# Preparing the edge slots of a message-passing layer: conversion loop without chunk restarts, paired records, transposes on TensorE

## The reference

```python
for l in range(5):
    h = leaky(x @ W1[l] + b1[l]) @ W2[l] + b2[l]
    e = leaky(edge_attr @ We1[l] + be1[l]) @ We2[l] + be2[l]
    msg = h[src] * e * dot_scale[l]
    agg = segment_sum(msg, dst, num_segments=n)
    x = layernorm(x + agg * res_w[l]) * ln_g[l] + ln_b[l]
```

## Time and profile before

| what | value |
|---|---|
| median of 3 runs | 6804.82 us (6796.08 to 6816.65) |
| the profiled execution's own time | 6786.73 us, its span 6784.7 us |
| busy in the span | PE 85%, PEld 56%, DVE 76%, ACT 17%, POOL 67% |
| TensorE clock granted, mean | 0.884 of 2.4 GHz |
| conversion stage | from 799.8 us (first fetch) to 1290.9 us (first load of the layers) |

### The profile page before, as it was taken

The page is one execution under the profiler, slowest core; times in us unless marked ns, Lnnn a source line. Parts: engine busy times, 40 slices in busy tenths (PEclk is TensorE's granted clock), DMA queues, the critical chain, the costliest instruction groups (busy, mean ns, idle before and its releaser), DMA issues.

```text
span 6784.7 us, 172226 instructions
## 1 busy us (share of the span) xinstructions
PE 5734.0 (85%) x64844; PEld 3820.2 (56%) x64845; DVE 5152.1 (76%) x7991; ACT 1160.8 (17%) x1852; POOL 4527.7 (67%) x4793
## 2 busy tenths in 40 slices
PE   6776888888888888988878988887888887888887
PEld 2223443456666655666655666665566665556665
DVE  8997533588877678877758887766887775888886
ACT  0000232211111111111111111211111122111111
POOL 5777777466666457766737776754777672777775
PEclk8997566899989889999979999997999997999998
DMA  3112388755556445555635555553555563556664
GB/s 132 25 25 49 92 212 210 185 134 135 139 136 148 115 113 127 145 136 142 149 84 136 139 139 142 148 136 91 133 141 137 144 149 89 137 145 148 156 172 111
DMA packets 733557, 886.39 MB, mean 131 GB/s; under 512 B 325488, under 2 KB 502976, under 8 KB 731568
## 3 DMA queue, kind: packets, MB, share of 16 engines
q1 hardware_dynamic: 568480, 703.64, 39.7%
q0 software_dynamic: 152144, 154.93, 11.5%
q10 hardware_dynamic: 12096, 16.53, 0.8%
HBM read 749.51 MB, written 125.06 MB: 129 GB/s over the span
## 4 chain that ended last, share of the span: by engine, by line
PE 46%; issue 18%; DVE 16%; POOL 12%; DVEq 4%; ACT 3%; DMA 1%; ACTq 0%; SPq 0%; POOLq 0%
PE bank L976 14%; POOL slots L775 11%; PE bank L972 9%; PE bank L1025 7%; PE bank L1050 5%; DVE arena L1659 3%; PE bank L854 3%; PE bank L1012 3%; DVEq L1779 2%; DVE arena L1667 2%; DVE arena L1747 2%; ACT arena L1238 2%; PE bank L840 2%; DVE x_packed L1667 2%; DVE nodes_state L1715 2%
## 5 line engine op out<-in xcount | busy, mean ns | idle before, releaser
L788 POOL DMA_INDIRECT arena<-h_rows,src x3855 | 3676.5, 954 | 1798.9 <-issue 1258.4
L976 PEld LDWEIGHTS bank<-w2s,arena 128*128 128x128 f32 x8960 | 1188.5, 212 | 779.6 <-DVE arena L1747 421.8
L976 PE MATMUL bank<-w2s,arena 128*128 128x128 f32 x8960 | 1321.1, 305 | 201.0 <-DVE arena L1747 186.0
L775 POOL DMA_INDIRECT slots<-arena,slot_index x792 | 785.6, 992 | 267.1 <-issue 241.2
L972 PE MATMUL bank<-nodes_state,edge_w 64*128 64x512 f32 x980 | 617.9, 714 | 305.5 <-DVE nodes_state L1715 142.3
L1050 PEld LDWEIGHTS bank<-arena 112*64 112x64 f32 x20160 | 657.4, 141 | 269.2 <-issue 246.7
L1050 PE MATMUL bank<-arena 112*64 112x64 f32 x20160 | 744.0, 228 | 61.4 <-issue 55.3
L972 PE MATMUL bank<-x_packed,edge_w 64*128 64x512 f32 x1260 | 760.7, 686 | 16.9 <-ACT std L1187 15.9
L1238 ACT ACTIVATE arena<-bank,tenth 128x512 f32<-128x512 f32 x490 | 336.4, 687 | 2416.4 <-PE bank L972 2416.1
L1659 DVE SCALAR_TENSOR_TENSOR arena<-bank,edge_w,arena 128x512 f32<-128x512 f32 x490 | 366.6, 748 | 435.3 <-ACT arena L1238 430.4
L1667 DVE TENSOR_TENSOR x_packed<-bank,slot_rel 128x2880 f32<-128x2880 f32 (+8 forms) x315 | 588.8, 1869 | 15.9 <-issue 15.9
(11 more groups left out here) (198 smaller groups left out, 5811.7 us busy)
## 6 DMA issues: line engine op xcount, KB each, us to landing
arena<-slot_pick SPq DMA_DIRECT2D x630, 448.0 KB
arena<-h_rows SPq DMA_DIRECT2D x630, 224.0 KB
x_packed<-slot_attr SPq DMA_DIRECT2D x630, 128.0 KB
nodes_state<-attr_t SPq DMA_DIRECT2D x485, 128.0 KB
arena<-h_rows,src POOLq DMA_INDIRECT x3855
slot_pick<-arena SPq DMA_DIRECT2D x126, 448.0 KB
slots<-arena SPq DMA_DIRECT2D x9, 1904.0 KB, 22.1
arena<-slots SPq DMA_DIRECT2D x126, 136.0 KB
```

Of the source, the lines that this page charges most:

```text
L775: pool.indirect_dma_start(slots, bass.IndirectOffsetOnAxis(ap=slot_index[:, t:t + 1], axis=0), records[:, v, j, :], None).then_inc(record_ ...
L788: pool.indirect_dma_start(to[0:n, at:at + D], None, table, bass.IndirectOffsetOnAxis(ap=index[0:n, t:t + 1], axis=0)).then_inc(landed(t), 16)
L976: mm = pe.matmul(to[:, j * P:(j + 1) * P], acts[:, j * TILE:(j + 1) * TILE], w2s[:, :], start=True, stop=True)
```

## The change

The conversion runs through all 126 groups as one loop on SP and on PE. SP issues three fetches, then for each group `keep_hot(p)` and behind it the fetch of group p + 3; the wait for POOL's records stands ahead of the first fetch of each chunk. There are four record buffers in place of six. In a buffer the records have a pitch of 64 floats, with record j of side 0 and record j of side 1 next to each other, so that one 98-float slice holds both; a fetch is two DMAs of 512 records, one for each side. PE turns such a slice with one `transpose` of 128 x 98 into partitions 0 to 97, four for each group. ACT copies the 98 partitions with one instruction. DVE clears `msg` once at the start, since the gaps between records are now turned and copied as well.

```diff
-RECORD_BUFS = 6
+RECORD_BUFS = 4
+        PAIR = D + REC
+        slot_records = arena[:, records_at:records_at + RECORD_BUFS * HALF].rearrange(
+            "p (v j r) -> p v j r", v=RECORD_BUFS, r=P)
+        by_side = slot_records.rearrange("p v j (side r) -> p v side j r", side=2)
...
-                    sp.dma_start(slot_records[:, v, :, :],
-                                 slots[p * GROUP:(p + 1) * GROUP, :].rearrange("(t q) r -> q t r", q=TILE)
-                                 ).then_inc(slots_landed[v], 16)
+                    for side in range(2):
+                        at = p * GROUP + side * HALF
+                        sp.dma_start(by_side[:, v, side, :, 0:REC],
+                                     slots[at:at + HALF, :].rearrange("(j q) r -> q j r", q=TILE)
+                                     ).then_inc(slots_landed[v], 16)
...
-                    first_p, last_p = c * BG, (c + 1) * BG
-                    for p in range(first_p, first_p + RECORD_BUFS - 1):
-                        fetch(p)
-                    for p in range(first_p, last_p):
-                        if p + RECORD_BUFS - 1 < last_p:
-                            fetch(p + RECORD_BUFS - 1)
-                        keep_hot(p)
+                for p in range(RECORD_BUFS - 1):
+                    fetch_sent(p)
+                for p in range(NB):
+                    keep_hot(p)
+                    if p + RECORD_BUFS - 1 < NB:
+                        fetch_sent(p + RECORD_BUFS - 1)
...
                     for j in range(TPH):
-                        for side in range(2):
-                            mm = pe.matmul(turn_ps[p % 2][side * D:side * D + REC, j * TILE:(j + 1) * TILE],
-                                           slot_records[:, v, side * TPH + j, :], ident[:, :], start=True, stop=True)
+                        mm = pe.transpose(turn_ps[p % 2][0:PAIR, j * TILE:(j + 1) * TILE],
+                                          slot_records[:, v, j, 0:PAIR], ident[:, :])
                     mm.then_inc(turn_ready, 1)
...
-                for c in range(CHUNKS):
-                    turn(c * BG)
-                    for p in range(c * BG, (c + 1) * BG):
-                        if p + 1 < (c + 1) * BG:
-                            turn(p + 1)
-                        source_of(p)
+                turn(0)
+                for p in range(NB):
+                    if p + 1 < NB:
+                        turn(p + 1)
+                    source_of(p)
...
-                    for side in range(2):
-                        at = slice(side * D, side * D + REC)
-                        ins = act.activation(turned[at, p % 2, :], turn_ps[p % 2][at, :], ACT.Identity)
-                    ins.then_inc(turned_out, 1)
+                    act.activation(turned[0:PAIR, p % 2, :], turn_ps[p % 2][0:PAIR, :], ACT.Identity
+                                   ).then_inc(turned_out, 1)
...
+            dve.memset(area("msg"), 0.0)
...
-                    dve.tensor_copy(slot_rel[:, p * TPG:(p + 1) * TPG], slot_records[:, v, :, ED + 1]
-                                    ).then_inc(rel_taken, 1)
+                    dve.tensor_copy(slot_rel[:, p * TPG:(p + 1) * TPG].rearrange("p (side j) -> p side j", side=2),
+                                    by_side[:, v, :, :, ED + 1]).then_inc(rel_taken, 1)
```

More of the change, by code:

```diff
@@ L277, in build @@
         start_f = area("slot_pick", 2 * NG, 2 * NCA)
-        slot_records = arena[:, first_of["hid_tenth"]:first_of["hid_tenth"] + RECORD_BUFS * TPG * REC].rearrange(
-            "p (v t r) -> p v t r", v=RECORD_BUFS, r=REC)
+        PAIR = D + REC
+        records_at = first_of["hid_tenth"]
+        slot_records = arena[:, records_at:records_at + RECORD_BUFS * HALF].rearrange(
+            "p (v j r) -> p v j r", v=RECORD_BUFS, r=P)
+        by_side = slot_records.rearrange("p v j (side r) -> p v side j r", side=2)
+        assert records_at + RECORD_BUFS * HALF == total
         spill_records = spill_msg[:, 0:TPG * REC].rearrange("p (t r) -> p t r", r=REC)
@@ L615, in keep_hot, with fetch_sent @@
                     sp.dma_start(slot_pick[p, :, :], source_hot[0:ROWS, p % 2, :]).then_inc(hot_stored[p % 2], 16)
-                for c in range(CHUNKS):
[L618 to L623, removed]
-                    first_p, last_p = c * BG, (c + 1) * BG
-                    for p in range(first_p, first_p + RECORD_BUFS - 1):
-                        fetch(p)
-                    for p in range(first_p, last_p):
-                        if p + RECORD_BUFS - 1 < last_p:
-                            fetch(p + RECORD_BUFS - 1)
-                        keep_hot(p)
+                def fetch_sent(p):
+                    if p % BG == 0:
+                        n = records_of(p // BG)
+                        for v in range(2):
+                            sp.wait_ge(record_sent[v], 16 * REC_TILES * ((n + 1 - v) // 2))
+                        if p == (CHUNKS - 1) * BG:
+                            sp.dma_start(spill_records,
+                                         slots[SPILL:SPILL + GROUP, :].rearrange("(t q) r -> q t r", q=TILE)
+                                         ).then_inc(spill_landed, 16)
+                    fetch(p)
+                for p in range(RECORD_BUFS - 1):
[4 more added lines that the diff above has]
+                        fetch_sent(p + RECORD_BUFS - 1)
                 for v in range(2):
@@ L890, in turn @@
                     v = p % RECORD_BUFS
-                    pe.wait_ge(slots_landed[v], 16 * (p // RECORD_BUFS + 1))
+                    pe.wait_ge(slots_landed[v], 32 * (p // RECORD_BUFS + 1))
                     if p > 1:
@@ L1578, in turn_slots @@
                     v = p % RECORD_BUFS
-                    dve.wait_ge(slots_landed[v], 16 * (p // RECORD_BUFS + 1))
-                    dve.tensor_copy(slot_rel[:, p * TPG:(p + 1) * TPG], slot_records[:, v, :, ED + 1]
-                                    ).then_inc(rel_taken, 1)
+                    dve.wait_ge(slots_landed[v], 32 * (p // RECORD_BUFS + 1))
+                    dve.tensor_copy(slot_rel[:, p * TPG:(p + 1) * TPG].rearrange("p (side j) -> p side j", side=2),
+                                    by_side[:, v, :, :, ED + 1]).then_inc(rel_taken, 1)
                     if p > 1:
```

## The result

| | before | changed |
|---|---|---|
| median of 4 runs | 6800.73 us | 6906.02 us (6900.44 to 6924.61) |
| ratio | 1 | 1.0165, 95% interval 1.0136 to 1.0195 |
| profiled execution, own time | 6786.73 us | 6924.61 us |
| first to last `keep_hot` | 477.9 us | 616.8 us |
| clock granted, mean | 0.884 | 0.865 |

The account below looks back on a forecast made before the run. The conversion's loop was taken as the bound: PE at the low clock, DMA at the upper, plus restarts. Changed, 125 groups at 4.54 us add 86.6 us; with the memset, 6804.8 + 87.5 = 6892 us, range 6790 to 6955.

Parts of the forecast that it names:

- The loop, 9.09 us: Conversion: one-hots of p, store, fetch landing, turn, source matmuls, DVE, one-hots of p + 2; 9.09 us for two groups.
- Two of the signs: Expected in the changed trace: `keep_hot` at an even 4.5 us; PE idle for records before the transposes in nearly every group.
- The pace, 4.54 us: Conversion at the lower clock: 4.54 us a group, from 9.09 us for two, with a fetch landing in 4.11.
- Transposes, 0.97 us for four: PE's turn of a group: four transposes at 0.24 us each, 0.97 in all, bounds 0.48 and 1.89.
- ACT's copy at nothing: ACT in the conversion: one copy for two changes the time by 0, as the copy is covered by a whole turn.
- Restarts, -64 us: Eight chunk boundaries of the conversion: running on across them removes 64 us, if the pace inside the chunks stayed.
- Memset, +0.9 us: DVE's clearing of `msg` at the head of its chain adds 0.9 us.
- POOL's gate: SP's wait for POOL's records before a chunk's fetches costs nothing; it would bite below 3.05 us a group for chunk 6.
- The clock at 0.50: PE's clock in the conversion stays at its lower level, 0.50, through the whole stage.
- the one on the other side, faster: Rival: fetches land in 2.9 us and the clock is high, 3.23 us a group, -76 us, 6729 us; chance 0.16.
- The dear transposes: Rival: transposes cost as much as full matmuls, turn 1.89 us, 5.0 us a group, 6950 us; chance 0.13.
- the high clock: Rival: PE's clock stays high in the conversion, 3.84 us a group, 6805 us, no change; chance 0.13.

Follow-up runs that it names:

- a3_matmul: The changed kernel with the old eight identity matmuls and two ACT copies in place of the transposes: stage 635.0 us, ratio 1.0174 to the kernel before.
- a1_order: The changed kernel with fetch(p + 3) issued ahead of `keep_hot(p)`: stage 414.7 us, 3.32 a group, ratio 0.9935 to the kernel before.
- a7_warm: The changed kernel with three matmuls of no use added to each group on PE: stage 581.3 us, ratio 1.0115 to the kernel before.
- b1_through_2: The kernel before with only the chunk restarts taken out of SP's and PE's loops, run again in more rounds: stage 448.4 us, ratio 0.9994.
- b1_through: The kernel before with only the chunk restarts taken out of SP's and PE's loops, first run: stage 404.3 us, ratio 0.9998.

## Why the prediction was right

The direction, the mechanism and the size came out: 6906 against 6892, in the range. By its steps:

- **The loop, 9.09 us.** Measured 9.13 in the timeline above, term by term: 0.42, landing 4.12 (4.11 forecast from the boundaries), turn 1.03 (0.97), source 2.15, DVE 1.41. One edit at each of the loop's handles moved the stage as it should: order, depth, store, turn. Shown. Two of the signs came otherwise than I had said: the `keep_hot`s aren't even but in pairs of 3.02 and 6.1 us, and PE stands idle for records in 72 of some 120 groups, not in nearly every one. The loop of two groups allows both, since only its sum is fixed.
- **The pace, 4.54 us: too low.** In the profiled execution it was 5.12 while POOL was sending (66 intervals) and 4.72 after (59). The term that was mis-sized is the landing. The mean over eight boundaries was right for a good turn, but in the run there are landings of 6 to 7 us, where the longest at the boundaries was 4.99. The longest and one more of them:

```profile
814.21 6.52 DMA arena<-slots
...
1105.53 7.15 DMA arena<-slots
```

  These are pieces of the chain in the changed kernel; a piece starts some 0.4 us after the issue. All six pieces over 6 us fall in the time of POOL's sends, and the longest after it is 5.19; that POOL's small writes are their cause is argued from this, not shown. 0.39 us a group too little makes 49 us in that trace, where the last `keep_hot` came at 1430.2 us in place of 1375. The forecast meets the median more closely (105 us against 87.5) in part because the traced execution is the slowest of the four; the others have no trace, so how their remaining 18 us divide isn't known.
- **Transposes, 0.97 us for four** (bounds 0.48 and 1.89): 1.09. The Trainium skill's 275 ns for a transpose ("TensorE: Matmul & The Clock Gate", Part 4), given for bf16, fits these float32 ones at the lower clock. Its rule that they don't count as work for the clock isn't borne out or refuted: with matmuls in their place (a3_matmul), at 5.08 us a group, the clock was as low, 0.51.
- **ACT's copy at nothing**: right. One copy takes 0.60 us, and `source_of` of the same group comes a whole turn later, as said.
- **Restarts, -64 us**: they are gone, with no gap of the old kind left, and the loop's waits stand in their place. As a gain by itself the term holds only at the high clock. I had let the pace inside the chunks stand; without the restarts it was 3.23 us at a clock of 0.78 and 3.59 at 0.55, so the stage gained 75 or 31 us, and no total showed either.
- **Memset, +0.9 us**: 0.91 in the trace. The stage began 4.0 us later, though (803.8 against 799.8); the other 3.1 weren't looked into.
- **POOL's gate**: 1.5 us of waits, as forecast nothing.
- **The clock at 0.50**: right over the whole stage of the changed kernel. The kernel before was not as low as the one row of 50 us that I had shown: 0.68 in the mean over its stage, which with two levels of 0.50 and 1.00 makes about a third of the time at the upper one. So its 3.31 us a group were a mixture of both paces, and part of what the change loses is the upper level. How large a part wasn't measured; a1_order shows that the loss goes away without the upper level coming back.

Of the rivals, the one on the other side, faster, needed landings of 2.9 us and a high clock, and had neither. The dear transposes (1.09 us in place of 1.89) and the high clock (0.50) fell too.

## What to carry to other kernels

When a load is moved behind a store that waits for results, count the loop: store's wait, load's landing, and the work to the next result, divided by the number of groups it spans. Here a ring of four with the load behind made that two groups and 4.6 us; one swapped line or four more buffers brought 3.3. Removing visible gaps is worth their sum only if the pace between them has room: an overlapped loop takes on whichever bound the gaps were hiding.

## What the hardware showed that I had not expected

- The same programs took 11.1 to 11.5 ms on three other chips, against 6.8. The conversion was as fast as ever (479.6 us), the stage before it took 1466 us in place of 800. There DVE and PE stand idle much longer between instructions that need each other's results; from the kernel before, the same lines of ranking, first on the fast chip, then on a slow one:

```profile
300.43 1.02 PE L873 MATMUL bank<-arena,ones 128*128 128x448 f32 x2 [0.19 <-DVE arena L1414]
...
302.09 0.62 DVE L1414 TENSOR_TENSOR arena<-arena 128x448 f32<-128x448 f32 x1
302.63 0.61 DVE L1420 TENSOR_REDUCE x_packed<-arena 128x4 f32<-128x448 f32 x1
302.76 0.30 PEld L873 LDWEIGHTS bank<-arena,ones 128*128 128x128 f32 x2 [0.92 <-DVE arena L1414]
```

```profile
303.70 0.62 DVE L1405 TENSOR_TENSOR arena<-arena,bank 128x448 f32<-128x448 f32 x1 [8.23 <-remote]
...
304.91 0.50 PEld L873 LDWEIGHTS bank<-arena,ones 128*128 128x128 f32 x2 [8.45 <-issue]
304.91 1.86 PE L873 MATMUL bank<-arena,ones 128*128 128x448 f32 x2 [7.09 <-issue]
```

  DVE's instructions are as long (0.62 us); the matmul's two records take 1.86 us in place of 1.02, at a clock of 0.50 in place of 1.00 in the window from 299.9 to 306 us. The idle time before them grew most: 8.45 us in place of 0.92 for the weight load, 7.09 in place of 0.19 for PE, and 8.23 for DVE. The slow trace names no instruction that ended it, only `remote` and `issue`. The cause is open. A difference of 1% in one stage is hard to see in such a total, which is why the stages were compared.
- PE's busy share did not tell the clock. At 95% (332.83 of 350 us, a7_warm) it had 0.53, and at 99% (347.31, b1_through_2) 0.55, while at 94% (329.59, b1_through) it had 0.78.
- Turning 98 columns of 128 records by a float32 transpose takes 0.27 us at the lower clock (four in 1.09), against 0.48 for the two matmuls of 34 columns that it replaces (eight in 1.93).
